# Quantised FFN, first half: groups of four batches in pairs, Gelu over 1,024 columns, row normalisation and quantisation on GpSimd

## The chip, the cores and the metric

The kernel runs on one core of a Trainium2 chip. The metric is the device time of one launch in microseconds; lower is better.

## What is computed

Two layers of a gated cross-attention block over x of 64 x 128 x 128, each an attention and a feed-forward part. The change is in the feed-forward part of the first layer, which works on quantised numbers:

```python
def quantize_a16(x):
    amax = jnp.clip(jnp.max(jnp.abs(x)), 1e-08, None)
    scale = 32767.0 / amax
    x_q = jnp.clip(jnp.round(x * scale), -32768.0, 32767.0) / scale
    return _ste(x, x_q)
W_in_sim = quantize_w8_per(W_in, axis=0)
W_out_sim = quantize_w8_per(W_out, axis=1)
x_sim = quantize_a16(x)
hidden = jax.nn.gelu(x_sim @ W_in_sim + b_in, approximate=False)
hidden_sim = quantize_a16(hidden)
out = hidden_sim @ W_out_sim + b_out
...
x = x + jnp.tanh(g_ffn[0]) * _L0_ffn_ref(_layernorm(x, axis=-1), L0_ffn_W_in, L0_ffn_b_in, L0_ffn_W_out, L0_ffn_b_out)
```

The scale of `hidden` is taken over all of it. So the whole of hidden (512 x 8,192 numbers) must be there before any of it can be quantised, and the part has two halves.

## The kernel before, in words

X, 64 batches of 128 rows by 128 channels, stays in SBUF with rows on the partitions. `quantised_ffn` treats it as 16 groups (`GROUPS`) of four batches (`GROUP`), 512 columns each. There are no loops at run time here: every engine has its own written-out program, and semaphores alone tie them together. Names of the helpers are used below for what they issue.

The **first half** makes HID, `[128, 16, 4, 512]`, the hidden values with their 512 features in four chunks (`FC`) of 128 partitions. For each group g:

- GpSimd, `normalise(g)`: two operations over 512 columns, X minus the row means (`mv`) and times the row's inverse deviation (`rs`), into XN[g % 2] (L1260, L1263). It waits until `quantise(g-2)` has read that buffer.
- VectorE, `quantise(g)`: times the scale `sx`, plus the constant ROUND, which rounds, into XQ[g % 2] (L1386).
- TensorE, `turn(g)`: four transposes into the PSUM bank pX[g % 2] (L1287).
- ScalarE, `high(g)`: a rounded bf16 copy HI of the bank (L1338). VectorE, `low(g)`: the bf16 rest LO (L1392).
- TensorE: for each chunk c two matmuls of 512 columns, W_in by HI and by LO, into the PSUM bank pU[c] (L1304, L1305). One bank per chunk: chunk c of a group waits for the Gelu of the same chunk a group before.
- ScalarE: Gelu with bias and scale from pU[c] into HID (L1351), 512 columns.
- VectorE, `largest(g)`: the largest magnitude of the group's 2,048 columns per partition, into amax (L1397). The last group's is taken chunk by chunk (L1423).

The orders are these. TensorE: turn(g+1), then the four chunks of g. ScalarE: high(g+1), then four Gelus. VectorE: low(g+1), quantise(g+2), largest(g-1). Behind group 1 TensorE also transposes eight blocks of the weights of the second layer's feed-forward part (L1310, L1311). `keep_busy` issues matmuls without use.

After the last group VectorE takes the maximum over amax, TensorE spreads it (`across(1)`) and VectorE makes the scale `sh`. The **second half** quantises HID, multiplies by W_out (L1328) and adds to X. The change leaves it as it is, save that its banks pD now are the two halves of pU[0].

At the start of the stage VectorE finds the largest normalised value from per-row statistics (L1400 to L1404), `across(0)` spreads it and `scale_from(sx)` makes the scale (L1379 to L1381). GpSimd's first `normalise` waits for the third of these steps (`step_`, 3). The five loads of the next attention layer's weights are issued by SyncE at the start.

HALVES is one buffer of 2 x 2,048 columns for XN, XQ, HI, LO and the raw weights; in the second half it holds HQ.

## Time and profile before

| | before |
|---|---|
| median of 3 runs | 1488.27 us (1488.05 to 1488.7) |
| span of the profiled execution | 1487.2 us |
| TensorE busy | 1444.1 us (97%) |
| VectorE busy | 1064.9 us (72%) |
| ScalarE busy | 923.1 us (62%) |
| GpSimd busy | 640.4 us (43%) |

The profiled execution's span runs from its first to its last instruction; the runs' time has about a microsecond around it. The stage of the change stands from 616.2 us to 737.7 us of the span, its first half up to 677.1 us. A row of the timeline gives the start and the length of an instruction, or of several merged ones with their count (x4). Instructions of one engine overlap at their ends, so what one costs in a queue is the distance from its start to the next one's. A bracket tells how long the engine stood idle before it and what released it. PE is TensorE, PEld its weight load, DVE VectorE, ACT ScalarE, POOL GpSimd. The tiles XN, XQ, HI and LO all read HALVES, pX reads u_px and pU reads u_pu.

### The profile page before, as it was taken

What the parts mean: (1) busy time and instruction counts of PE and PEld (TensorE: products, weight loads), DVE (VectorE), ACT (ScalarE), POOL (GpSimd) and SP (SyncE); (2) the same over time, 40 slices, a digit from 0 to 9 for tenths busy, and PEclk for the clock granted to TensorE, in tenths of its full rate; (3) what the DMA queues carried; (4) which work ended last, traced back from release to release, by engine and by line L of the source; (5) the groups of instructions that cost most, each with busy time, mean ns of one, the idle gap of its engine ahead of it and who ended that gap; (6) DMA issues with size and microseconds to landing.
All of it is one profiled execution on the core that took longest, in us unless ns stands there. A gap on an engine that the chain in (4) does not pass through costs nothing. (4 is left out here: it accounts for less than half of the span.)

```text
span 1487.2 us, 27490 instructions
## 1 busy us (share of the span) xinstructions
PE 1444.1 (97%) x9366; PEld 1209.9 (81%) x9384; DVE 1064.9 (72%) x2311; ACT 923.1 (62%) x1924; POOL 640.4 (43%) x755
## 2 busy tenths in 40 slices
PE   9999999999999999879999999999999999999997
PEld 8888888888888887639978888888888888778886
DVE  5677877666767678798566666666767676776887
ACT  4666666666666665496456666666666666556663
POOL 1333344343433334556023434343333333455885
PEclk9999999999999999999999999999999999999999
DMA  7655544444444442300055444444444444320011
GB/s 226 192 178 161 165 132 153 137 145 144 140 146 138 153 130 85 91 1 1 12 183 165 135 157 133 157 129 161 134 159 132 154 129 151 109 79 8 29 35 43
DMA packets 202786, 182.70 MB, mean 123 GB/s; under 512 B 12368, under 2 KB 201808, under 8 KB 202640
## 3 DMA queue, kind: packets, MB, share of 16 engines
q1 hardware_dynamic: 202080, 180.91, 38.7%
q8 instruction: 73, 1.20, 0.3%
q14 instruction: 57, 0.47, 0.1%
q10 hardware_dynamic: 576, 0.13, 0.1%
HBM read 95.74 MB, written 85.25 MB: 122 GB/s over the span
## 5 line engine op out<-in xcount | busy, mean ns | idle before, releaser
L1131 POOL TENSOR_TENSOR PN<-E,RC 128x512 f32<-128x512 f32 x378 | 331.2, 904 | 491.9 <-DVE RC L1089 491.9
L1038 DVE TENSOR_REDUCE MX<-pS 128x6 f32<-128x462 f32 (+1 forms) x384 | 222.6, 580 | 265.4 <-PE pS L657 265.4
L772 ACT ACTIVATE G<-pP 128x308 f32<-128x308 f32 (+1 forms) x488 | 208.9, 428 | 226.8 <-PE pP L525 226.5
L695 PE MATMUL pO<-work,PT 128*128 128x128 f32 (+1 forms) x2560 | 328.3, 276 | 4.1 <-ACT PT L856 4.1
L657 PE MATMUL pS<-G,XT 128*128 128x462 f32 (+1 forms) x768 | 321.0, 507 | 0.0
L695 PEld LDWEIGHTS pO<-work,PT 128*128 128x128 f32 (+1 forms) x2560 | 307.7, 192 | 8.4 <-issue 5.8
L847 ACT ACTIVATE E<-E 128x462 f32<-128x462 f32 (+1 forms) x384 | 209.6, 546 | 136.5 <-DVE E L1048 128.2
L523 PE MATMUL pP<-Chi,Ahi 128*128 128x308 f32 x496 | 235.2, 474 | 1.4 <-ACT G L772 1.2
L1048 DVE TENSOR_TENSOR E<-pS,MX 128x462 f32<-128x462 f32 (+1 forms) x384 | 223.6, 582 | 8.9
L856 ACT ACTIVATE PT<-pT 128x512 f32<-128x512 f32 (+1 forms) x384 | 200.2, 522 | 30.2 <-PE pT L680 28.7
L1086 DVE TENSOR_REDUCE SM<-E 128x16 f32<-128x1232 f32 (+1 forms) x144 | 184.8, 1290 | 44.7 <-ACT E L847 43.6
L680 PE MATMUL pT<-ident,PN 128*128 128x128 f32 (+1 forms) x1280 | 198.7, 273 | 3.7 <-ACT PT L856 3.7
L778 ACT ACTIVATE ST<-pP 128x512 f32<-128x512 f32 x290 | 172.0, 593 | 39.3 <-PE pP L536 36.6
L680 PEld LDWEIGHTS pT<-ident,PN 128*128 128x128 f32 (+1 forms) x1280 | 156.2, 138 | 23.1 <-ACT PT L856 6.0
L657 PEld LDWEIGHTS pS<-G,XT 128*128 128x128 f32 x768 | 137.4, 189 | 32.7 <-issue 15.1
L534 PE MATMUL pP<-Bhi,Vhi 128*128 128x512 f32 x300 | 149.6, 499 | 3.1 <-PEq L160 1.7
L524 PE MATMUL pP<-Chi,Alo 128*128 128x308 f32 x496 | 150.8, 304 | 0.0
L525 PE MATMUL pP<-Clo,Ahi 128*128 128x308 f32 x496 | 150.7, 304 | 0.0
L523 PEld LDWEIGHTS pP<-Chi,Ahi 128*128 128x128 f32 x496 | 94.3, 190 | 30.9 <-issue 21.0
L536 PE MATMUL pP<-Bhi,Vlo 128*128 128x512 f32 x300 | 118.2, 394 | 0.0
L535 PE MATMUL pP<-Blo,Vhi 128*128 128x512 f32 x300 | 118.1, 394 | 0.0
L524 PEld LDWEIGHTS pP<-Chi,Alo 128*128 128x128 f32 x496 | 94.6, 191 | 27.7 <-issue 21.0
(241 smaller groups left out, 2032.7 us busy)
## 6 DMA issues: line engine op xcount, KB each, us to landing
values<-ST SPq DMA_DIRECT2D x256, 256.0 KB
work<-values SPq DMA_DIRECT2D x512, 128.0 KB
values<-ST SPq DMA_DIRECT2D x64, 208.0 KB
work<-values SPq DMA_DIRECT2D x128, 104.0 KB
C<-in_ctx SPq DMA_DIRECT2D x32, 154.0 KB
X<-in_x SPq DMA_DIRECT2D x16, 256.0 KB, 5.0
out<-s_O SPq DMA_DIRECT2D x16, 256.0 KB, 2.3
work<-in_L_xattn_Wq SPq DMA_DIRECT2D x2, 512.0 KB, 5.9
```

The costliest lines, as they stand in the source:

```text
L523: nc.tensor.matmul(out, p["Ahi"][:, head, :], hi, start=True, stop=False)
L524: nc.tensor.matmul(out, p["Alo"][:, head, :], hi, start=False, stop=False)
L657: nc.tensor.matmul(out, XT[:, half, b, :], G[:, half, b, h0:h1, :].rearrange("p h k -> p (h k)"), start=True, stop=True).then_inc(score_re ...
L680: last = nc.tensor.transpose(pT[n % 2][0:rows, c - c0, :], PN[(t - 1) % 2][:, start:start + rows], p["ident"][:, :])
L695: last = nc.tensor.matmul(pO[:, 0:CH], PT[0:rows, c, :], V[(t - 1) % VRING][0:rows, tile, CH * hh:CH * hh + CH], start=c == 0, stop=c == C ...
L772: return nc.scalar.activation(G[0:live, g % 2, :, head, :], bank[0:live, 0:KEYCOLS].rearrange("p (b k) -> p b k", k=KEYS), ACT.Copy)
L847: nc.scalar.activation(e, e, ACT.Exp).then_inc(exp_done, 1)
L856: nc.scalar.activation(PT[0:rows, c0:c1, :], pT[n % 2][0:rows, 0:c1 - c0, :], ACT.Copy).then_inc(p_out, 1)
L1038: nc.vector.tensor_reduce(MX[:, h0:h1], pS[u][:, 0:(h1 - h0) * KEYS].rearrange("p (h k) -> p h k", k=KEYS), X_AXIS, ALU.max).then_inc(max_ ...
L1048: nc.vector.tensor_tensor(E[t % 2][:, h0:h1, :], pS[u][:, 0:(h1 - h0) * KEYS].rearrange("p (h k) -> p h k", k=KEYS), MX[:, h0:h1].unsqueez ...
L1086: last = nc.vector.tensor_reduce(SM[:, h0:h1], E[t % 2][:, h0:h1, :], X_AXIS, ALU.add)
L1131: nc.gpsimd.tensor_tensor(out, e, scale, ALU.mult).then_inc(prob_ready, 1)
```

## The change

The first half goes by pairs of groups, eight of them (`PAIRS`).

- GpSimd's `normalise(g)` is four operations, one per batch, of 128 columns: X plus `minus` (the means, negated once at the start) times `rs`, both read per partition. `quantise(g)` goes to GpSimd too, in place in XQ. Its order: rows of groups 0 and 1, then, after the scale is there, quantise 0 and 1, then rows and quantise of one group after the other. `normalise(g)` waits for turn(g-2).
- TensorE turns groups 0 and 1 first. For each pair a chunk is four matmuls (HI and LO of both groups) into one of two tiles pU[c % 2] of 1,024 columns. A chunk waits for the Gelu two chunks before. Behind chunk 0 stand the turns of the next pair.
- ScalarE's Gelu is over 1,024 columns. Behind the first Gelu of a pair stand both `high` of the next.
- VectorE: both `low` of pair j, then `largest` of both groups of pair j-2. The last pair is reduced chunk by chunk over 1,024 columns.
- HI and LO have four buffers each, XN is gone.

```diff
-        XN = [half_of(0, i, 1).rearrange("p (b d) -> p b d", d=CH) for i in range(2)]
-        XQ = [half_of(0, 2 + i, 1).rearrange("p (b d) -> p b d", d=CH) for i in range(2)]
-        HI = [half_of(1, i, 1).bitcast(BF16)[:, 0:512] for i in range(2)]
+        XQ = [half_of(0, i, 1).rearrange("p (b d) -> p b d", d=CH) for i in range(2)]
+        parts = [half_of(0, 2, 1), half_of(0, 3, 1), half_of(1, 0, 1), half_of(1, 1, 1)]
+        HI = [h.bitcast(BF16)[:, 0:512] for h in parts]
...
-        pU = [s.enter_context(nc.psum_tensor(f"u_pu{i}", [128, 512], F32)) for i in range(FC)]
+        pU = [s.enter_context(nc.psum_tensor(f"u_pu{i}", [128, 2, 512], F32)) for i in range(2)]
...
@@ GpSimd @@
-                if g >= 2:
-                    pool.wait_ge(xq_ready, g - 1)
-                nc.gpsimd.tensor_tensor(XN[half], p["X"][:, rows, :], p["mv"][:, rows, 0:1].to_broadcast([128, GROUP, CH]),
-                                        ALU.subtract).then_inc(centred, 1)
-                pool.wait_ge(centred, g + 1)
-                nc.gpsimd.tensor_tensor(XN[half], XN[half], p["rs"][:, rows].unsqueeze(2).to_broadcast([128, GROUP, CH]),
-                                        ALU.mult).then_inc(xn_ready, 1)
+                if g >= 2:
+                    pool.wait_ge(xq_turned, g - 1)
+                for b in range(GROUP):
+                    t = g * GROUP + b
+                    last = nc.gpsimd.tensor_scalar(XQ[g % 2][:, b, :], p["X"][:, t, :], minus[:, t:t + 1],
+                                                   p["rs"][:, t:t + 1], ALU.add, ALU.mult)
+                last.then_inc(xn_ready, 1)
+
+            def quantise(g):
+                pool.wait_ge(xn_ready, g + 1)
+                nc.gpsimd.tensor_scalar(XQ[g % 2], XQ[g % 2], sx[:, 0:1], ROUND, ALU.mult, ALU.add).then_inc(xq_ready, 1)
 
             nc.gpsimd.sem_clear(range(min(p["spent"]), max(p["spent"]) + 1))
+            nc.gpsimd.tensor_scalar(minus[:, :], p["mv"][:, :, 0], -1.0, 0.0, ALU.mult, ALU.add).then_inc(turned_sign, 1)
             pool.wait_ge(step_, RANGE - 1)
-            for g in range(GROUPS):
+            pool.wait_ge(turned_sign, 1)
+            normalise(0)
+            normalise(1)
+            pool.wait_ge(step_, RANGE + SCALE)
+            quantise(0)
+            quantise(1)
+            for g in range(2, GROUPS):
                 normalise(g)
+                quantise(g)
@@ TensorE @@
             turn(0)
-            for g in range(GROUPS):
-                if g + 1 < GROUPS:
-                    turn(g + 1)
-                pe.wait_ge(hi_out, g + 1)
-                pe.wait_ge(lo_out, g + 1)
+            turn(1)
+            for j in range(PAIRS):
+                for g in (2 * j, 2 * j + 1):
+                    pe.wait_ge(hi_out, g + 1)
+                    pe.wait_ge(lo_out, g + 1)
                 for c in range(FC):
-                    wait(pe, gelu_done, g * FC + c - FC + 1)
+                    wait(pe, gelu_done, j * FC + c - 1)
                     f = slice(128 * c, 128 * c + 128)
-                    nc.tensor.matmul(pU[c][:, :], WIN[:, f], HI[g % 2], start=True, stop=False)
-                    nc.tensor.matmul(pU[c][:, :], WIN[:, f], LO[g % 2], start=False, stop=True).then_inc(up_ready, 1)
-                if g == 1:
+                    for i in range(2):
+                        nc.tensor.matmul(pU[c % 2][:, i, :], WIN[:, f], HI[(2 * j + i) % 4], start=True, stop=False)
+                        last = nc.tensor.matmul(pU[c % 2][:, i, :], WIN[:, f], LO[(2 * j + i) % 4], start=False, stop=True)
+                    last.then_inc(up_ready, 1)
+                    if c == 0 and j + 1 < PAIRS:
+                        turn(2 * j + 2)
+                        turn(2 * j + 3)
+                if j == 0:
@@ ScalarE @@
-            for g in range(GROUPS):
-                if g + 1 < GROUPS:
-                    high(g + 1)
+            for j in range(PAIRS):
                 for c in range(FC):
-                    act.wait_ge(up_ready, g * FC + c + 1)
-                    nc.scalar.activation(HID[:, g, c, :], pU[c][:, :], ACT.Gelu, bias=b_in[:, c:c + 1],
+                    act.wait_ge(up_ready, j * FC + c + 1)
+                    nc.scalar.activation(HID[:, 2 * j:2 * j + 2, c, :], pU[c % 2][:, :, :], ACT.Gelu, bias=b_in[:, c:c + 1],
                                          scale=in_scale[:, c:c + 1]).then_inc(gelu_done, 1)
+                    if c == 0 and j + 1 < PAIRS:
+                        high(2 * j + 2)
+                        high(2 * j + 3)
@@ VectorE @@
-            for g in range(GROUPS):
-                if g + 1 < GROUPS:
-                    low(g + 1)
-                if g + 2 < GROUPS:
-                    quantise(g + 2)
-                if g >= 1:
-                    largest(g - 1)
+            for j in range(1, PAIRS):
+                low(2 * j)
+                low(2 * j + 1)
+                if j >= 2:
+                    largest(2 * j - 4)
+                    largest(2 * j - 3)
+            for g in range(GROUPS - 4, GROUPS - 2):
+                largest(g)
             for c in range(FC):
-                dve.wait_ge(gelu_done, (GROUPS - 1) * FC + c + 1)
-                last = nc.vector.tensor_reduce(amax[:, GROUPS - 1 + c:GROUPS + c], HID[:, GROUPS - 1, c, :],
-                                               X_AXIS, ALU.max, apply_absolute_value=True)
+                dve.wait_ge(gelu_done, (PAIRS - 1) * FC + c + 1)
+                last = nc.vector.tensor_reduce(amax[:, GROUPS - 2 + c:GROUPS - 1 + c], HID[:, GROUPS - 2:GROUPS, c, :],
+                                               mybir.AxisListType.XY, ALU.max, apply_absolute_value=True)
```

The order of the instructions shows it at two places. On VectorE, after the scale is made, there stood before (L1386 `quantise`, L1392 `low`, L1397 `largest`, L1408 and L1413 small operations):

```order
L1386 TENSOR_SCALAR HALVES<-HALVES,sx 128x512
L1408 TENSOR_SCALAR in_scale<-inv,sx 128x4
L1386 TENSOR_SCALAR HALVES<-HALVES,sx 128x512
L1392 SCALAR_TENSOR_TENSOR HALVES<-u_px,HALVES 128x512
L1413 TENSOR_SCALAR gbias_f<-brow_f,gate_f 128x128
L1392 SCALAR_TENSOR_TENSOR HALVES<-u_px,HALVES 128x512
L1386 TENSOR_SCALAR HALVES<-HALVES,sx 128x512
L1392 SCALAR_TENSOR_TENSOR HALVES<-u_px,HALVES 128x512
L1386 TENSOR_SCALAR HALVES<-HALVES,sx 128x512
L1397 TENSOR_REDUCE amax<-HID 128x1
```

and now (L1407 is `low`, L1412 `largest`):

```order
L1422 TENSOR_SCALAR in_scale<-inv,sx 128x4
L1407 SCALAR_TENSOR_TENSOR HALVES<-u_px,HALVES 128x512 x2
L1427 TENSOR_SCALAR gbias_f<-brow_f,gate_f 128x128
L1407 SCALAR_TENSOR_TENSOR HALVES<-u_px,HALVES 128x512 x4
L1412 TENSOR_REDUCE amax<-HID 128x1 x2
L1407 SCALAR_TENSOR_TENSOR HALVES<-u_px,HALVES 128x512 x2
```

The first `largest` stood behind low(0) to low(2), and stands behind low(0) to low(5). On TensorE, from the first turns to chunk 1 of the first pair (L1300 `turn`, L1318 and L1319 the chunks' matmuls, by HI and by LO):

```order
L1300 MATMUL u_px<-ident,HALVES 128x128 x8
L1318 MATMUL u_pu<-HALVES,WIN 128x512
L1319 MATMUL u_pu<-HALVES,WIN 128x512
L1318 MATMUL u_pu<-HALVES,WIN 128x512
L1319 MATMUL u_pu<-HALVES,WIN 128x512
L1300 MATMUL u_px<-ident,HALVES 128x128 x8
L1318 MATMUL u_pu<-HALVES,WIN 128x512
L1319 MATMUL u_pu<-HALVES,WIN 128x512
```

Before, all eight matmuls of group 0 stood ahead of the third turn; now the third and the fourth turn stand ahead of chunk 1.

## Rows read from the trace of the kernel before

**Rows 1.** Windows: start:end, us, busy us of PE, PEld, DVE, ACT, POOL, PEclk, DMA

```profile
620.00:623.50 3.50, 1.28 (x8) 0.83 (x8) 3.49 (x5) 1.05 (x3) 3.34 (x4) 1.00 1.01 304
624.10:627.20 3.10, 3.10 (x11) 1.46 (x10) 1.84 (x2) 2.88 (x5) 2.66 (x3) 0.50 1.20 298
640.00:650.00 10.00, 7.54 (x39) 3.70 (x38) 10.00 (x10) 10.00 (x18) 6.61 (x8) 1.00 0.01 2
```

**Rows 2.** Timeline of one group: start us, us, engine, line, operation

```profile
647.36 0.68 DVE L1392 SCALAR_TENSOR_TENSOR HALVES<-u_px,HALVES 128x512 bf16<-128x512 f32 x1
647.96 0.48 DVE L1386 TENSOR_SCALAR HALVES<-HALVES,sx 128x512 f32<-128x512 f32 x1
648.35 2.28 DVE L1397 TENSOR_REDUCE amax<-HID 128x1 f32<-128x2048 f32 x1
...
649.49 0.83 ACT L1338 ACTIVATE HALVES<-u_px 128x512 bf16<-128x512 f32 x1
...
649.97 3.03 ACT L1351 ACTIVATE HID<-u_pu,b_in,in_scale 128x512 f32<-128x512 f32 x4
...
650.55 0.68 DVE L1392 SCALAR_TENSOR_TENSOR HALVES<-u_px,HALVES 128x512 bf16<-128x512 f32 x1
```

**Rows 3.** Timeline, the end of the first half

```profile
668.80 5.84 ACT L1351 ACTIVATE HID<-u_pu,b_in,in_scale 128x512 f32<-128x512 f32 x8
...
670.26 4.47 DVE L1397 TENSOR_REDUCE amax<-HID 128x1 f32<-128x2048 f32 x2
...
674.65 2.46 DVE L1423 TENSOR_REDUCE amax<-HID 128x1 f32<-128x512 f32 x4
```

**Rows 4.** Waits, 619 to 675: who waited for whom, us in total, times, longest

```profile
POOL HALVES L1260 <- DVE HALVES L1386: 11.7, 12, 1.0
```

**Rows 5.** ScalarE's groups by shape (busy us, mean ns), and the Gelus' ns min/median/max

```profile
L1365 ACT ACTIVATE HALVES<-HID 128x2048 f32<-128x2048 f32 x15 | 28.7, 1914 | 22.5 <-PE u_pu L1328 22.3 <-DVE HID L1437 0.2
...
L1360 ACT ACTIVATE HALVES<-HID 128x512 f32<-128x512 f32 x4 | 2.2, 620 | 3.6 <-DVE HID L1433 3.6
...
L1351 ACT ACTIVATE HID<-u_pu,b_in,in_scale x64: 772/1016/1206, 624.2 to 673.4; 128x512 f32<-128x512 f32 x64
```

**Rows 6.** Timeline, the start of the first half

```profile
617.20 1.04 POOL L1260 TENSOR_TENSOR HALVES<-X,mv 128x512 f32<-128x512 f32 x1 [1.30 <-DVE up L1403]
...
619.53 1.11 DVE L1386 TENSOR_SCALAR HALVES<-HALVES,sx 128x512 f32<-128x512 f32 x1
...
620.70 0.42 PEld L1287 LDWEIGHTS u_px<-ident,HALVES 128*128 128x128 f32 x4 [1.29 <-DVE HALVES L1386]
...
621.39 0.60 ACT L1338 ACTIVATE HALVES<-u_px 128x512 bf16<-128x512 f32 x1 [0.93 <-PE u_px L1287]
...
622.74 0.68 DVE L1392 SCALAR_TENSOR_TENSOR HALVES<-u_px,HALVES 128x512 bf16<-128x512 f32 x1
...
624.20 3.33 ACT L1351 ACTIVATE HID<-u_pu,b_in,in_scale 128x512 f32<-128x512 f32 x4
...
628.24 0.69 DVE L1392 SCALAR_TENSOR_TENSOR HALVES<-u_px,HALVES 128x512 bf16<-128x512 f32 x1 [2.12 <-ACT HALVES L1338]
```

**Rows 7.** Timeline, two matmuls of 512 columns at the full clock

```profile
649.20 0.38 PE L1305 MATMUL u_pu<-HALVES,WIN 128*128 128x512 bf16 x1
...
649.41 0.38 PE L1304 MATMUL u_pu<-HALVES,WIN 128*128 128x512 bf16 x1
```

**Rows 8.** GpSimd: timeline of three casts, and groups by shape (busy us, mean ns)

```profile
35.43 0.40 POOL L140 CAST Vhi<-Chi 128x256 fp32r<-128x256 f32 x1 [8.54 <-DVE Clo L127]
35.78 0.23 POOL L145 CAST Vhi<-Chi 128x52 fp32r<-128x52 f32 x1
35.95 0.41 POOL L140 CAST Vlo<-Clo 128x256 fp32r<-128x256 f32 x1
...
L1263 POOL TENSOR_TENSOR HALVES<-HALVES,rs_after 128x512 f32<-128x512 f32 x16 | 16.8, 1047 | 1.3
...
L1119 POOL TENSOR_TENSOR RS<-VE,half 128x4 f32<-128x4 f32 x32 | 32.3, 1009 | 171.1 <-DVE VE L926 171.1
```

More of the change, by code:

```diff
@@ L1213, in quantised_ffn @@
         brow = sb("brow_f0", [128, CH])
-        amax = sb("amax", [128, GROUPS - 1 + FC])
+        PAIRS = GROUPS // 2
+        amax = sb("amax", [128, 2 * (PAIRS - 1) + FC])
+        minus = sb("minus", [128, BATCH])
         def half_of(i, first, n):
             return HALVES[:, i, 512 * first:512 * (first + n)]
-        XN = [half_of(0, i, 1).rearrange("p (b d) -> p b d", d=CH) for i in range(2)]
-        XQ = [half_of(0, 2 + i, 1).rearrange("p (b d) -> p b d", d=CH) for i in range(2)]
-        HI = [half_of(1, i, 1).bitcast(BF16)[:, 0:512] for i in range(2)]
-        LO = [half_of(1, i, 1).bitcast(BF16)[:, 512:1024] for i in range(2)]
+        XQ = [half_of(0, i, 1).rearrange("p (b d) -> p b d", d=CH) for i in range(2)]
+        parts = [half_of(0, 2, 1), half_of(0, 3, 1), half_of(1, 0, 1), half_of(1, 1, 1)]
+        HI = [h.bitcast(BF16)[:, 0:512] for h in parts]
+        LO = [h.bitcast(BF16)[:, 512:1024] for h in parts]
         raw_fc = half_of(1, 2, 1).rearrange("p (c d) -> p c d", d=CH)
@@ L1227, in quantised_ffn @@
         pX = [s.enter_context(nc.psum_tensor(f"u_px{i}", [128, 512], F32)) for i in range(2)]
-        pU = [s.enter_context(nc.psum_tensor(f"u_pu{i}", [128, 512], F32)) for i in range(FC)]
+        pU = [s.enter_context(nc.psum_tensor(f"u_pu{i}", [128, 2, 512], F32)) for i in range(2)]
         pF = s.enter_context(nc.psum_tensor("pF", [128, 512], F32))
         pP = s.enter_context(nc.psum_tensor("pP", [128, 512], F32))
-        pD = pU[0:2]
+        pD = [pU[0][:, i, :] for i in range(2)]
         gate_in, bias_in, up_bias_in, raw_in, raw_turned, fhi_out = (
             sem(n) for n in ("gate_in", "bias_in", "up_bias_in", "raw_in", "raw_turned", "fhi_out"))
-        centred, xn_ready, xq_ready, xq_turned, hi_out, lo_out, up_ready, gelu_done = (
-            sem(n) for n in ("centred", "xn_ready", "xq_ready", "xq_turned", "hi_out", "lo_out", "up_ready", "gelu_done"))
+        turned_sign, xn_ready, xq_ready, xq_turned, hi_out, lo_out, up_ready, gelu_done = (
+            sem(n) for n in ("turned_sign", "xn_ready", "xq_ready", "xq_turned", "hi_out", "lo_out", "up_ready", "gelu_done"))
         step_, spread, tanh, scaled, gbias_made, biased = (
@@ L1335, in high @@
                 act.wait_ge(xq_turned, g + 1)
-                if g >= 2:
-                    act.wait_ge(up_ready, (g - 1) * FC)
-                nc.scalar.activation(HI[g % 2], pX[g % 2][:, :], ACT.Copy, bias=-ROUND).then_inc(hi_out, 1)
+                if g >= 4:
+                    act.wait_ge(up_ready, (g // 2 - 1) * FC)
+                nc.scalar.activation(HI[g % 4], pX[g % 2][:, :], ACT.Copy, bias=-ROUND).then_inc(hi_out, 1)
             act.wait_ge(gate_in, 16)
@@ L1381, in scale_from @@
                 done(nc.vector.reciprocal(s[:, 0:1], s[:, 1:2]))
-            def quantise(g):
-                dve.wait_ge(xn_ready, g + 1)
-                wait(dve, xq_turned, g - 1)
-                nc.vector.tensor_scalar(XQ[g % 2], XN[g % 2], sx[:, 0:1], ROUND, ALU.mult, ALU.add).then_inc(xq_ready, 1)
             def low(g):
                 dve.wait_ge(hi_out, g + 1)
-                if g >= 2:
-                    dve.wait_ge(up_ready, (g - 1) * FC)
-                nc.vector.scalar_tensor_tensor(out=LO[g % 2], in0=pX[g % 2][:, :], scalar=ROUND, in1=HI[g % 2],
+                if g >= 4:
+                    dve.wait_ge(up_ready, (g // 2 - 1) * FC)
+                nc.vector.scalar_tensor_tensor(out=LO[g % 4], in0=pX[g % 2][:, :], scalar=ROUND, in1=HI[g % 4],
                                                op0=ALU.subtract, op1=ALU.subtract).then_inc(lo_out, 1)
             def largest(g):
-                dve.wait_ge(gelu_done, (g + 1) * FC)
+                dve.wait_ge(gelu_done, (g // 2 + 1) * FC)
                 nc.vector.tensor_reduce(amax[:, g:g + 1], HID[:, g, :, :].rearrange("p c n -> p (c n)"),
@@ L1406, in _ @@
             scale_from(sx)
-            quantise(0)
             nc.vector.tensor_scalar(in_scale[:, :], inv[:, 0, :], sx[:, 1:2], None, ALU.mult).then_inc(scaled, 1)
-            quantise(1)
             low(0)
+            low(1)
             dve.wait_ge(tanh, 1)
```

2 lines of the change are left out of this document (1 added, 1 removed).

## Prediction

> **What bounds the stage now.** The first view is the windows by stretch [rows 1]: from 640 to 650 us VectorE and ScalarE are both busy for all of 10.00 us, TensorE for 7.54 and GpSimd for 6.61. So it has two candidates, and the timeline of one group [rows 2] decides between them. On VectorE one group is `low` (starts 647.36), `quantise` (647.96), `largest` (648.35) and the next `low` (650.55): 0.60 + 0.39 + 2.20 = 3.19 us, without a gap. On ScalarE the next group's `high` starts at 649.49 and its first Gelu at 649.97, so a `high` takes 0.48; Gelus start 0.66 apart where nothing holds them (eight in 5.84 us from 668.80 [rows 3], less 1.21 for the last one's own length, by 7), so a group needs 0.48 + 4 x 0.66 = 3.12. VectorE bounds by 0.07 us, and ScalarE stands right behind it. The waits [rows 4] agree: GpSimd's rows waited 11.7 us for VectorE's `quantise`. The end [rows 3] matters as much: after the last `low` VectorE still has `largest` for groups 13 and 14 (from 670.26) and four quarters of group 15 (from 674.65, 2.46 us together), done at 677.11, and everything behind the stage starts from there. The second half is left alone by the change: it runs out of the same HID, on TensorE, and its transfers were sent long before. A microsecond saved before 677.11 is thus a microsecond of the whole.
>
> **VectorE's work.** Removed: 14 of the 16 `quantise` lie in the loop, at 0.39 each. A pair costs 2 x 0.60 + 2 x 2.20 = 5.60 us, against 6.38. The last pair's four reductions are now over 1,024 columns: 2,048 columns take 2.20 and 512 take 0.60 from start to start, 1.04 ns a column, so 1.13 each. From the start of low(4) on, VectorE has 12 x 0.60 + 14 x 2.20 + 4 x 1.13 + 0.1 for the last one's tail = 42.6 us, and it can't be done before that.
>
> **ScalarE's work.** The copy of 2,048 columns takes 1,914 ns and that of 512 takes 620 [rows 5]: 0.84 ns a column. 512 more columns on a Gelu so add 0.43 to 0.66: 1.09. A pair is 4 x 1.09 + 2 x 0.48 = 5.32, against 6.24.
>
> **TensorE's ring.** Before, a chunk of pU was rewritten four Gelus later; now there are two tiles, so chunk c waits for Gelu c-2. From low's end (622.74 + 0.68) to the first Gelu (624.20) [rows 6] a chunk of two matmuls took 0.78; two more at 0.22 [rows 7] make 1.2, of which about 0.1 is the release. A Gelu of 1,024 lasts 0.77 + 0.43 = 1.20 from start to release (0.77 is the shortest of 512 columns, in the line's rows [rows 5]). Release to release is then (1.20 + 1.1) / 2 = 1.15, not 1.09, where no `high` stands between. With three such steps ScalarE and TensorE need about 5.5 per pair. This still is under VectorE's 5.60.
>
> **GpSimd's work** is the term that the trace doesn't show. Casts of 256 and 52 columns start 0.35 and 0.17 apart [rows 8]: 0.88 ns a column and 0.12 fixed. A 128-column row is at least 0.24, a 512-column `quantise` at least 0.57. The two-input operation took 1.047 for 512 [rows 8]: 1.80 ns a column, so 0.36 and 1.05. I take 0.36 for a row, because it reads two per-partition operands as well, and 0.80 for `quantise`, midway. The far end is the power of four columns, 1.01 [rows 8]: an operation can cost that whatever its width. A pair takes 8 x 0.36 + 2 x 0.80 = 4.5 us (3.1 to 5.0 with the near bounds), hidden under 5.6. Its slack is 1.1; if that goes, `turn` is late and with it everything. The negation of 64 means (about 0.2) stands before the wait on the deviations and is free while they come.
> The Trainium skill (GPSIMD Engine Reference, Performance versus the Vector engine) gives a loop of 1.03 cycles per element up to two operations and about 1.8 beyond, and advises VectorE for elementwise work. By 1.8 cycles a row would be 0.12 + 0.19 = 0.31 and `quantise` 0.89, an estimate from that page; the sum would be the same to 0.2 us.
>
> **The start.** This is where the change pays. All rows of two groups now come before the first `quantise`. GpSimd starts at 617.20 [rows 6]; 8 x 0.36 bring it to 620.1, and the scale has been there since 619.5, when VectorE began its own `quantise`, which ended at 620.64. Two `quantise` end at 620.9 and 621.7. From there turn to `high` 0.69 (620.70, 621.39), `high` 0.60, `low` 0.68, chunk 1.2, handovers 0.1: first Gelu at 624.9, against 624.20: **+0.7**.
> TensorE's order is now chunk 0, then the turns of groups 2 and 3, then chunk 1. GpSimd has them at 621.7 + 2 x (4 x 0.36 + 0.80) + 0.2 for handovers = 626.4. The second turn (0.42) and chunk 1 (1.1) follow: second Gelu at 627.9, 3.0 after the first instead of 2.1. Then Gelus 2 and 3, and the eight transposes of the spiking weights (0.85) stand before pair 1: first Gelu of pair 1 at 632.0. high(4) starts 1.09 later and low(4) 0.65 after that: 633.7. VectorE's first `largest` stands behind low(4) and low(5), though its group is done by 631.6; it has nothing to do from 627 to 633.7. Now it is never idle after 628.24 [rows 6]. End: 633.7 + 42.6 = 676.3, against 677.11: **-0.8 us**.
>
> **The clock.** From 624.1 to 627.2 the granted clock was 0.50, the 1.2 GHz level, after TensorE had been busy for only 1.28 us of the 3.5 from 620 to 623.5 [rows 1], for want of quantised groups. It hardly does more there after the change. If the same stretch is slow again, the first chunk's tail, the turns and chunk 1 take twice as long: four matmuls 0.86 more at either chunk, of which 1.3 us reach low(4). End 677.6, **+0.5 us**. The trace decides for neither, so I put the stage between them: **-0.3 us**. The Trainium skill (TensorE: Matmul & The Clock Gate, What's actually happening) says that activity releases the throttle and lack of it sets it, which speaks for the second value.
>
> The sum is made in the profiled execution, whose span is 1487.2; the median of the runs is 1488.27, 1.1 around it. Forecast: 1488.27 - 0.3 = **1488.0 us**. A measurement of this kernel can tell about 0.2%, 3.0 us, from no change.
>
> **Rivals.**
> - *The saving arrives in full.* VectorE gets low(4) early enough and pays only its work. From 628.24 it then loses 12 x 0.39 = 4.7 us: 1483.6. For it: 11.7 us of waits for `quantise` go [rows 4]. Against it: the order puts the first `largest` behind low(5), and that needs pair 0 finished on ScalarE.
> - *GpSimd becomes the bound.* Place: the rows and `quantise` of a pair, released only by the turns of the pair before. Price: at 0.55 a row, 8 x 0.55 + 2 x 0.80 = 6.0, with two handovers 6.1 per pair. The start slips 3.0 us (8 rows, then 8 more before Gelu 1), and five pairs lose 0.5 each: -0.8 + 3.0 + 2.7 = +4.9, 1493.2. It decides from 0.49 a row on, where 8 rows and two `quantise` fill 5.5. For it: the 1.01 us of four columns; against it: casts are far below. By the Trainium skill's advice on that page this is what moving elementwise work to GpSimd invites; no row here shows it.
> - *The clock stays low through pair 0* because TensorE's work comes in pieces with waits for GpSimd between. Chunks then pass at 1.6 us instead of 1.15 until about 631: 1.1 more on top of the +0.5, 1489.9.
> - *A Gelu of 1,024 saves nothing* (1.32): ScalarE keeps 6.24 per pair and is the bound: +1.9 to +3, about 1490.5. Against it: the fixed part in the copies [rows 5].
>
> **Chances.** Forecast with either clock 0.58 (its own range 1485.6, by 0.24 and 0.57 on GpSimd at full clock, to 1489.0); full saving 0.13; GpSimd bound 0.19; clock low for longer 0.06; Gelu 0.04. The range takes in the forecast's range, part of the full saving and GpSimd up to 0.55 a row: 1484.8 to 1493.5, with 0.1 left out on either side. Faster by over 0.2%: 0.13 and the lower edge of the forecast, 0.16. Slower: 0.19 and half of the last two, 0.24. Within: 0.60.
>
> **What would show it.** Right: `low` and `largest` back to back from low(4) to the end, 5.6 per pair; Gelus 1.1 to 1.2 apart; GpSimd idle about 1 us per pair, a row near 0.36; a VectorE gap of 5 us or more before low(4). Wrong: TensorE waiting for GpSimd's `quantise` in every pair (the second rival), `largest` of group 0 starting before 632 (the first), or a Gelu of 1,024 over 1.2 from start to start.

## The result: 2.0 us slower, where 0.3 us faster was forecast

| | before | changed kernel |
|---|---|---|
| median of 20 runs each, us | 1488.13 (1487.54 to 1489.1) | 1490.13 (1489.22 to 1493.17) |
| ratio, 95% interval | | 1.0015 (1.0009 to 1.0021) |
| profiled execution: time, span, us | 1488.7, 1487.2 | 1493.17, 1491.4 |

The time lies in the forecast's range (1484.8 to 1493.5) and by the median in its band of "within 0.2%", but its sign is wrong: the whole interval of the ratio lies above 1. The profiled execution is the longest of the 20, so its +4.2 us of span shows more than the typical loss; how the two go together is told below.

The page of the changed kernel gives the sums over the span. Neither they nor the chain of what ended last point at the stage:

```profile
PE 1448.6 (97%) x9384; PEld 1212.3 (81%) x9384; DVE 1054.5 (71%) x2294; ACT 917.6 (62%) x1892; POOL 646.0 (43%) x804
```

**The loop is as forecast.** The timeline from 646 us (start, length, engine and line, operation), beside [rows 2]:

```profile
646.47 1.07 ACT L1356 ACTIVATE HALVES<-u_px 128x512 bf16<-128x512 f32 x2
647.10 1.28 DVE L1407 SCALAR_TENSOR_TENSOR HALVES<-u_px,HALVES 128x512 bf16<-128x512 f32 x2
647.42 4.72 ACT L1368 ACTIVATE HID<-u_pu,b_in,in_scale 128x1024 f32<-128x1024 f32 x4
648.30 4.46 DVE L1412 TENSOR_REDUCE amax<-HID 128x1 f32<-128x2048 f32 x2
```

Four Gelus take 4.72, one alone 1.20 or 1.21, so they start 1.17 apart (forecast 1.15 for TensorE's ring). Two `low` and two `largest` fill a pair on VectorE without a gap. The windows, in the columns of [rows 1], show the room on GpSimd, and GpSimd's groups by shape (busy us, mean ns, idle before) show its price, the term that no row of before had:

```profile
640.00:650.00 10.00, 8.16 (x43) 3.88 (x42) 10.00 (x8) 9.93 (x12) 8.90 (x19) 1.00 0.00 0
```

```profile
L1263 POOL TENSOR_SCALAR HALVES<-X,minus,rs_after 128x128 f32<-128x128 f32 x64 | 27.9, 452 | 5.0 <-PE u_px L1300 4.6 <-DVE up L1418 0.3
L1269 POOL TENSOR_SCALAR HALVES<-HALVES,sx 128x512 f32<-128x512 f32 x16 | 11.1, 696 | 1.4
```

A row takes 0.43 from start to start (eight in 3.47 below), a `quantise` 0.68. A pair is 8 x 0.43 + 2 x 0.68 = 4.8 us on GpSimd, under the 5.6 of the others; GpSimd is busy 8.90 us of 10 and never ends a wait in the loop.

**The start** is later than forecast. Timeline from 616 us, against [rows 6]:

```profile
617.16 3.47 POOL L1263 TENSOR_SCALAR HALVES<-X,minus,rs_after 128x128 f32<-128x128 f32 x8 [0.25 <-DVE up L1418]
618.76 0.29 DVE L1399 TENSOR_REDUCE sx<-u_px 128x1 f32<-128x128 f32 x1 [1.45 <-PE u_px L1294]
620.60 1.37 POOL L1269 TENSOR_SCALAR HALVES<-HALVES,sx 128x512 f32<-128x512 f32 x2
626.17 1.21 ACT L1368 ACTIVATE HID<-u_pu,b_in,in_scale 128x1024 f32<-128x1024 f32 x1 [2.86 <-PE u_pu L1319]
627.27 0.71 PEld L1300 LDWEIGHTS u_px<-ident,HALVES 128*128 128x128 f32 x4 [0.77 <-POOL HALVES L1269]
630.14 3.54 ACT L1368 ACTIVATE HID<-u_pu,b_in,in_scale 128x1024 f32<-128x1024 f32 x3 [1.11 <-PE u_pu L1319]
634.21 1.20 ACT L1368 ACTIVATE HID<-u_pu,b_in,in_scale 128x1024 f32<-128x1024 f32 x1 [0.53 <-PE u_pu L1319]
635.93 0.69 DVE L1407 SCALAR_TENSOR_TENSOR HALVES<-u_px,HALVES 128x512 bf16<-128x512 f32 x1 [6.18 <-PE u_pu L1319]
```

The last row is low(4): VectorE stood idle 6.18 us before it, 17.17 us after the scale's first step (618.76). The forecast had 633.7 at full clock. The windows show one reason for the rest: the granted clock was 0.50, the 1.2 GHz level, up to 630. (`e4_start` below, at full clock, prices it at 1.3 us.)

```profile
624.00:626.00 2.00, 1.81 (x5) 0.82 (x6) 0.23 (x2) 0.00 (x0) 2.00 (x5) 0.50 1.18 317
628.00:630.00 2.00, 2.00 (x7) 0.83 (x6) 1.28 (x2) 0.60 (x1) 1.90 (x5) 0.50 0.36 88
```

**The end** holds what the forecast did not look at. Timeline of the changed kernel from 670 us, against [rows 3]:

```profile
670.97 4.40 PE L61 MATMUL u_px<-ident 128*128 128x128 f32 x38
673.82 4.59 DVE L1438 TENSOR_REDUCE amax<-HID 128x1 f32<-128x1024 f32 x4
678.44 0.17 DVE L1442 TENSOR_REDUCE peak<-amax 128x1 f32<-128x18 f32 x1
678.66 0.80 PE L1294 MATMUL u_px<-ident,peak 128*128 128x128 f32 x2 [3.29 <-DVE peak L1442]
679.25 5.33 PE L61 MATMUL u_px<-ident 128*128 128x128 f32 x24
684.37 0.87 PE L1346 MATMUL u_pu<-WOUT,HALVES 128*128 128x128 f32 x5
```

and in the kernel before, up to its first `W_out` matmul (L1328):

```profile
672.46 4.40 PE L61 MATMUL u_px<-ident 128*128 128x128 f32 x38
677.14 0.17 DVE L1427 TENSOR_REDUCE peak<-amax 128x1 f32<-128x19 f32 x1
677.37 0.49 PE L1281 MATMUL u_px<-ident,peak 128*128 128x128 f32 x2 [0.50 <-DVE peak L1427]
677.69 2.84 PE L61 MATMUL u_px<-ident 128*128 128x128 f32 x24
680.37 4.85 PE L1328 MATMUL u_pu<-WOUT,HALVES 128*128 128x128 f32 x42
```

L61 is `keep_busy`: matmuls on an identity, issued to hold the clock, whose result nobody reads. The 38 are the 19 calls that follow the last chunk, the 24 the 12 calls behind the spread. The first set lasts 4.40 us in both kernels, but starts 1.49 us earlier in the changed one, which reaches `peak` 1.30 us later. Then TensorE waits 3.29 us for VectorE's last reductions (0.50 us before the change), and the clock falls: in the changed kernel's windows

```profile
676.00:678.50 2.50, 0.00 (x0) 0.00 (x0) 2.46 (x4) 0.00 (x0) 0.00 (x0) 0.87 0.00 0
678.50:681.00 2.50, 2.34 (x11) 2.34 (x12) 1.44 (x6) 0.20 (x1) 0.00 (x0) 0.50 0.00 0
```

TensorE is idle to 678.66 and at 0.50 from 678.5 on. The same 24 matmuls take 5.33 us instead of 2.84, and the first `W_out` matmul stands behind them.

**The sum of the profiled execution.** From `sx` to `peak`: 678.44 - 618.76 = 59.68, against 677.14 - 618.82 = 58.32 before: +1.36. From `peak` to the next stage's first transpose, 743.11 - 678.44 = 64.67 against 738.97 - 677.14 = 61.83: +2.84. Together +4.2, the difference of the spans.

**How typical it is.** Each run has its mean granted clock over the whole program. Of the 20 runs of the changed kernel five stood at 0.995 or 0.996, at 1491.43 to 1493.17 us; fifteen at 0.997 or 0.998, at 1489.22 to 1490.78. When it was run again (`e11_after`), two of eleven kept 1.000: 1488.94 and 1488.96. The 33 runs of the kernel before beside the first experiments all lie at 0.998 or more, 1487.65 to 1489.39, without such an order. So most of the loss goes with the clock. The two runs at 1.000 are still some 0.6 us above the kernel before (1488.95 against 1488.3); two runs of a rounded mean don't show whether that is there without the clock, and `e5_both` below finds nothing left.

### The profile page after: what moved, and what is told of

Read it like the earlier page. It is cut to its first block and busy times, and to the rows that moved or that the text cites. A ratio compares the mean times of both kernels' runs of the same rounds, so it can differ in the third digit from the quotient of the medians.

```text
span 1491.4 us, 27491 instructions
## 1 busy us (share of the span) xinstructions
PE 1448.6 (97%) x9384; PEld 1212.3 (81%) x9384; DVE 1054.5 (71%) x2294; ACT 917.6 (62%) x1892; POOL 646.0 (43%) x804
```

## The experiments

Two theories at first. **End**: the loss is the clock that falls in TensorE's idle 3.3 us behind the last chunk. **Start**: the loss is the longer way to low(4), through GpSimd's `quantise` and TensorE's low clock. Later a third question: what had the change to give at all. All runs, with the median time of the kernel before on the same chip 1488.42 (`e1` to `e4`), 1488.18 (`e5` to `e8`) and 1488.32 (`e9` to `e12`), and its median span 1486.6, 1486.4 and 1486.5. The last two columns are from the one profiled execution of each, from the scale's first step to `peak` and from `peak` to the next stage's first transpose:

| run | median us | ratio to before (95%) | median span | profile: scale to `peak` | `peak` to next stage |
|---|---|---|---|---|---|
| kernel before | 1488.13 | | | 58.32 | 61.83 |
| changed kernel | 1490.13 | 1.0015 (1.0009, 1.0021) | 1488.3 | 59.68 | 64.67 |
| e11_after | 1490.55 | 1.0016 (1.0007, 1.0025) | 1488.8 | 58.47 | 63.45 |
| e1_busy | 1490.17 | 1.0009 (1.0, 1.0019) | 1487.6 | 59.62 | 61.83 |
| e12_busy | 1490.41 | 1.0008 (0.9999, 1.0017) | 1487.6 | 59.84 | 61.83 |
| e2_early | 1491.66 | 1.002 (1.0011, 1.0029) | 1489.9 | 58.46 | 63.46 |
| e3_vq | 1490.14 | 1.0011 (1.0002, 1.002) | 1488.4 | 57.73 | 61.83 |
| e4_start | 1489.83 | 1.0012 (1.0003, 1.0021) | 1487.7 | 58.38 | 64.54 |
| e5_both | 1488.23 | 1.0003 (0.9994, 1.0012) | 1486.4 | 58.45 | 61.82 |
| e6_stream | 1485.18 | 0.9986 (0.9977, 0.9995) | 1483.0 | 54.66 | 61.84 |
| e7_all | 1483.88 | 0.9971 (0.9961, 0.9981) | 1482.1 | 53.68 | 61.83 |
| e8_pool | 1488.41 | 1.0001 (0.9992, 1.001) | 1486.6 | 57.98 | 61.82 |
| e9_groups | 1486.25 | 0.9986 (0.9977, 0.9995) | 1484.5 | 55.82 | 61.87 |
| e10_bfill | 1488.48 | 1.0001 (0.9992, 1.001) | 1486.4 | 57.65 | 61.82 |

The time around the span was 1.8 us in most runs, but 2.1 to 2.5 in the median of `e1`, `e4`, `e6`, `e10` and `e12`. (The "about a microsecond" ahead of the prediction, and the prediction's 1.1, compare the span of one execution, whose time was 1488.7, with the median of others.) Where less than 1 us matters the median span is therefore read beside the time. The span has a scatter of its own too: what lies outside the two stretches of the last columns adds up to 1366.0 to 1367.1 us in the fourteen profiles, whatever the kernel. So the spans of single profiles can't settle 1 us; the two columns leave this scatter out.

### e1_busy and e12_busy: fill the hole at the end

```diff
-            keep_busy(nc, p, spare, 19)
+            keep_busy(nc, p, spare, 32)
```

> The changed kernel with 32 instead of 19 matmuls without use behind the last chunk, nothing else. Theory: VectorE still ends the first half at 678.4 us, so amax is not earlier, but TensorE now works until it is needed. The granted clock stays at the full level from 678.5 to 684 us (0.50 there in the changed kernel), the 12 matmuls behind the spread take 2.8 us and not 5.3, and the first matmul by W_out starts 2.5 to 2.8 us sooner. Median 1488.3 to 1488.8 us, and the runs lie closer together than the changed kernel's 1489.2 to 1493.2. Rival (the loss lies in the loop, where GpSimd or the ring of two PSUM tiles sets the pace): 1490.1, no change.

> The first run once more (32 matmuls without use at the end, nothing else), since its profile showed the clock full and its median did not move. Theory: the median lies 1 to 2 us below that of the changed kernel run beside it. Rival (the filling at the end helps only when the start is filled as well): equal within 0.5 us, as in the first set.

In the windows of `e1_busy` the clock at the end is full, and the timeline has the 24 matmuls back at their old length:

```profile
678.00:680.00 2.00, 1.59 (x15) 1.59 (x15) 1.21 (x6) 0.00 (x0) 0.00 (x0) 1.00 0.00 0
```

```profile
678.73 2.84 PE L61 MATMUL u_px<-ident 128*128 128x128 f32 x24
```

In this profile the fill does what it was meant for: TensorE is kept busy and the clock stays. From `peak` to the next stage it is 61.83 us again, as before the change. The table says the same of all the kernels: 61.8 to 61.9 us in the ten profiles that kept full clock behind `peak`, 63.4 to 64.7 in the four that lost it. The size in the time is less plain. The median hardly moved (1490.17 and 1490.41, where 1488.3 to 1488.8 was expected, and for the second 1 to 2 us below the changed kernel), the ratio fell by 0.0006 to 0.0008, and the median span by 0.7 and 1.2 us; no run was left at a clock of 0.996 or less. Two runs of the same edit gave the same median span, 1487.6, and I take about 1 us for it. By the time alone the rival, equal within 0.5 us, holds; the difference between the two is the time around the span, whose growth I can't explain.

### e4_start: fill the waits at the start

```diff
-            keep_busy(nc, p, spare, 4)
+            keep_busy(nc, p, spare, 12)
             turn(0)
             turn(1)
+            keep_busy(nc, p, spare, 5)
```

> The changed kernel with 8 more matmuls without use behind the first spread and 5 behind the second turn, so that TensorE does not stand idle before the first pair. Theory of the clock at the start: the granted clock stays full from 624 to 630 us (0.50 in the changed kernel), chunk 0 takes 1.2 and not 2.0 us, chunk 1 likewise, low(4) comes 1.3 us sooner and the end too: median 1488.6 to 1489.0. Rival (GpSimd's quantise of group 3 sets the start whatever the clock): the second Gelu moves by under 0.5 us.

```profile
624.00:626.00 2.00, 1.40 (x11) 1.02 (x11) 1.12 (x3) 0.20 (x1) 1.90 (x4) 1.00 1.13 330
628.00:630.00 2.00, 1.83 (x11) 1.12 (x12) 1.14 (x2) 0.87 (x2) 1.90 (x6) 1.00 0.78 188
678.00:680.00 2.00, 1.75 (x8) 1.75 (x9) 0.91 (x5) 0.00 (x0) 0.00 (x0) 0.50 0.00 0
```

These are its windows: full clock at the start, 0.50 still at the end. The timeline has low(4) 15.88 us after the scale instead of 17.17:

```profile
635.52 1.29 DVE L1408 SCALAR_TENSOR_TENSOR HALVES<-u_px,HALVES 128x512 bf16<-128x512 f32 x2 [5.34 <-PE u_pu L1320]
```

VectorE's work behind low(4) is the same 42.5 us (635.52 to 678.02; in the changed kernel 635.93 to 678.44), so all of the 1.3 us reaches `peak`: 58.38 us after the scale. The median span falls by 0.6 us. Again the profile shows the mechanism, and by the median spans it is worth 0.6 to 1.1 us alone, about half of the loss. The median time, 1489.83, missed the expected 1488.6 to 1489.0.

### e5_both: both holes

The two diffs above in one kernel.

> The changed kernel with both fillings of TensorE's idle stretches at once (8 and 5 matmuls without use at the start, 32 instead of 19 at the end). Theory: with the clock full throughout, the first half ends as long after the scale's first step as in the kernel before (58.3 to 58.4 us), and the second half starts undisturbed: median 1488.2 to 1488.8 us, runs within 1 us of each other. Rival (the scatter from 1489.2 to 1493.2 comes from something other than the clock at these two places, such as GpSimd's pace): the median stays at 1489.8 or above and the runs stay 2 us or more apart.

1488.23 beside 1488.18: nothing is left of the loss in the median. The median spans are equal, 1486.4. The windows of the stage show 1.00 everywhere. Since the interval of this ratio (up to 1.0012) overlaps those of the changed kernel (from 1.0009, and from 1.0007 in `e11_after`), the spans decide here: 1488.3 to 1488.8 without the fill, 1487.6 and 1487.7 with one, 1486.4 with both. The loss against the kernel before is the clock, at both ends of the stage, in about equal parts. One part of the expectation failed: the runs were to lie within 1 us of each other and are 2.7 us apart (1487.46 to 1490.17), two of them at a clock of 1.000 with 1489.2 and 1489.69. The kernel before scatters by 1.8 us beside them. So the scatter of single runs is in part something other than this clock; what, is open.

### e3_vq: the first two `quantise` back on VectorE

```diff
-            pool.wait_ge(step_, RANGE + SCALE)
-            quantise(0)
-            quantise(1)
...
+                if g == 2:
+                    pool.wait_ge(xq_ready, 2)
...
+            quantise(0)
             nc.vector.tensor_scalar(in_scale[:, :], inv[:, 0, :], sx[:, 1:2], None, ALU.mult).then_inc(scaled, 1)
+            quantise(1)
```

> The changed kernel with quantise of groups 0 and 1 given back to VectorE, which waits there. Theory (the start on GpSimd costs: 3.5 us of rows, 1.4 us of quantise): the first Gelu comes 0.5 to 1 us sooner than 626.2, the second 1 to 1.5 us sooner than 630.1, since GpSimd is at the rows of group 2 1.4 us earlier; low(4) at 634.6 to 635.2 and the end of the first half as much earlier. Median 1489.0 to 1489.6. Rival (the clock alone sets the start): under 0.3 us.

In its timeline low(4) comes 15.23 us after the scale (618.44), though the clock was at 0.50 from 624 to 626:

```profile
625.03 1.20 ACT L1367 ACTIVATE HID<-u_pu,b_in,in_scale 128x1024 f32<-128x1024 f32 x1 [2.71 <-PE u_pu L1318]
633.67 1.29 DVE L1410 SCALAR_TENSOR_TENSOR HALVES<-u_px,HALVES 128x512 bf16<-128x512 f32 x2 [5.34 <-PE u_pu L1318]
...
676.40 0.49 PE L1293 MATMUL u_px<-ident,peak 128*128 128x128 f32 x2 [3.31 <-DVE peak L1447]
676.72 2.84 PE L61 MATMUL u_px<-ident 128*128 128x128 f32 x24
```

Its first Gelu starts 6.59 us after the scale, that of the changed kernel 7.41. Its profiled execution, at 1487.79, happened to keep the full clock at the end; its runs spread from 1487.79 to 1491.73, with two at a clock of 0.996. The median, 1490.14, was expected at 1489.0 to 1489.6 and doesn't show the shorter start. The end's hole is still there to take it back, and the two runs at 0.996 are the slowest; but two runs at 0.999 took 1490.65 and 1490.93, so the clock doesn't order these runs, and why the median stands where it does is not shown. TensorE was idle for 3.31 us ahead of the second spread in this profile too, and the clock stayed at 1.00 behind it: such a stretch does not bring the clock down every time.

### e2_early: less work in VectorE's tail, a miss

The first pair was reduced by chunks ahead of low(4), so that every later `largest` would stand a pair nearer to its Gelus.

```diff
             for j in range(1, PAIRS):
+                if j == 2:
+                    for c in range(FC):
+                        dve.wait_ge(gelu_done, c + 1)
+                        nc.vector.tensor_reduce(amax[:, c:c + 1], HID[:, 0:2, c, :], mybir.AxisListType.XY, ALU.max,
+                                                apply_absolute_value=True)
                 low(2 * j)
                 low(2 * j + 1)
-                if j >= 2:
+                if j >= 3:
```

> The changed kernel with the two reductions of the first pair taken chunk by chunk ahead of low(4), where VectorE waited 6.2 us. Theory (VectorE's work behind low(4), 42.5 us, sets the end): low(4) stays at 635.9, the end of the first half comes 4.4 us sooner, at 674.0, TensorE's matmuls without use cover the gap again, the clock stays full: median about 1485.3 us, 0.2% faster than the kernel before. Rival (GpSimd or the ring sets the pace): the last Gelu already ends at 672.3, so up to 4 us could come from the order alone only if VectorE was the bound; if the pace is set elsewhere the end moves by under 1 us and the median stays at 1489 to 1490.

```profile
634.91 1.29 DVE L1407 SCALAR_TENSOR_TENSOR HALVES<-u_px,HALVES 128x512 bf16<-128x512 f32 x2 [0.83 <-ACT HALVES L1356]
640.49 1.29 DVE L1407 SCALAR_TENSOR_TENSOR HALVES<-u_px,HALVES 128x512 bf16<-128x512 f32 x2 [4.29 <-PE u_pu L1319]
646.08 1.28 DVE L1407 SCALAR_TENSOR_TENSOR HALVES<-u_px,HALVES 128x512 bf16<-128x512 f32 x2
```

The wait only moved: 4.29 us of idle VectorE came ahead of low(6), because nothing was put behind low(5) in the place of what was drawn forward. The lag of a pair at the end was unchanged, TensorE was idle for 3.3 us there as before, and the median is the worst of all. (Why it is above the changed kernel's is not shown; six of its eleven runs stood at 0.995 or 0.996.) One thing is learned: low(6) comes 5.58 us after low(4) although VectorE stood idle for 4.29 us between them, so the ring of ScalarE and TensorE sets 5.58 by itself. This is one interval; from 640.49 on VectorE is busy throughout. VectorE's own work in a pair is the same 5.58: the two are level, and VectorE can never make up in the loop what it is late by at the start.

### e6_stream and e7_all: VectorE takes each chunk when it is there

```diff
-                low(2 * j)
-                low(2 * j + 1)
-                if j >= 2:
-                    largest(2 * j - 4)
-                    largest(2 * j - 3)
...
+            for j in range(PAIRS):
+                if j + 1 < PAIRS:
+                    low(2 * j + 2)
+                    low(2 * j + 3)
+                for c in range(FC):
+                    n = j * FC + c
+                    dve.wait_ge(gelu_done, n + 1)
+                    last = nc.vector.tensor_reduce(amax[:, n:n + 1], HID[:, 2 * j:2 * j + 2, c, :],
+                                                   mybir.AxisListType.XY, ALU.max, apply_absolute_value=True)
```

`e6_stream` has this with the start of `e4_start` and 17 calls of `keep_busy` at the end; `e7_all` adds the edit of `e3_vq` and keeps 4 calls ahead of the first turn.

> As the run before, but VectorE reduces each pair chunk by chunk (1,024 columns) right behind the low of the next pair, so it never lags a pair behind; 17 matmuls at the end since the wait there is shorter. Theory (the end is set by VectorE's lag of four reductions of 2,048 columns, 8.8 us behind the last low): the last reduction now ends 1.3 to 2.5 us after the last Gelu, near 673.5, 3.5 us sooner than e5's: median 1484.7 to 1485.5. Rival (the ring of two tiles and ScalarE set the end): VectorE's last reduction would end no sooner, since the last Gelu ends at 672.3 in the changed kernel; then under 1 us.

> e6 with quantise of groups 0 and 1 on VectorE (and only 4 matmuls ahead of the first turn, 5 behind the second). Theory: the start is 1.3 to 1.9 us shorter, as the third run of the first set showed, and this adds to e6: median 1483.2 to 1484.2. Rival (the clock and the start are the same microsecond counted twice): no better than e6 by more than 0.5 us.

Timeline of `e6_stream`:

```profile
628.82 4.59 DVE L1431 TENSOR_REDUCE amax<-HID 128x1 f32<-128x1024 f32 x4
634.24 1.29 DVE L1408 SCALAR_TENSOR_TENSOR HALVES<-u_px,HALVES 128x512 bf16<-128x512 f32 x2 [0.84 <-ACT HALVES L1357]
635.45 4.59 DVE L1431 TENSOR_REDUCE amax<-HID 128x1 f32<-128x1024 f32 x4
...
663.95 9.09 DVE L1431 TENSOR_REDUCE amax<-HID 128x1 f32<-128x1024 f32 x8
673.08 0.19 DVE L1435 TENSOR_REDUCE peak<-amax 128x1 f32<-128x32 f32 x1
```

VectorE's idle 6 us ahead of low(4) now holds the first pair's four reductions, and behind the last `low` stand eight of 1.13 us instead of 8.8 + 4.6 us. A pair costs 5.70 us (639.95 and 645.65 are the next two `low`), 0.12 more than in the changed kernel, and still `peak` comes 54.66 us after the scale instead of 58.45 (`e5_both`). Its median is 1485.18 us, but three of its eleven runs took 1487.74 to 1489.21 at a clock of 0.999, which is not explained. With `quantise` on VectorE for the first two groups it is 53.68, and `e7_all` is at 1483.88 us (nine runs, 1482.92 to 1485.38), ratio 0.9971 (0.9961 to 0.9981), ahead of both kernels. So a time like the one that the forecast gave a chance of 0.13 (1483.6) can be reached, with three things that the change did not have: the streamed order (3.4 us of median span, `e5_both` to `e6_stream`), the first two `quantise` on VectorE (a further 0.9), and the fill of TensorE's holes.

### e8_pool and e9_groups: which part of the change gives it

`e8_pool` is the kernel before with the rows and `quantise` on GpSimd and nothing else; groups stay single, a Gelu has 512 columns.

```diff
-                if g + 2 < GROUPS:
-                    quantise(g + 2)
```

`e9_groups` adds the streamed reduction over 512 columns and 12 calls of `keep_busy` at the end.

> One part of the change alone, in the kernel before: rows by 128-column operations and quantise on GpSimd, with Gelu over 512 columns, four PSUM banks, orders of TensorE and ScalarE as before. Theory (what cost time is the pairing: two groups' rows, turns and lows ahead of the first Gelu, and VectorE's lag at the end): the first Gelu stays at 624.2, ScalarE is the bound at 3.12 per group, VectorE has 2.80, so it keeps up and the first half ends about 0.7 us after the last Gelu, at 674.0: median 1485.0 to 1485.8. Rival (GpSimd's share is what costs): slower than the kernel before by 1 us or more.

> No pairs at all: the kernel of the GpSimd part alone, with VectorE reducing each chunk of 512 columns of a group right behind the low of the next, and 12 instead of 19 matmuls without use at the end. It tells what the pairs are worth once the order of VectorE is the good one. Theory (ScalarE's 3.16 us per group is then all that is left; its last Gelu ends near 674.3): the first half ends about 675.0, 1.9 us sooner than without the new order: median 1486.2 to 1486.8, 1 to 1.5 us behind the paired kernel in that order (1485.2). Rival (the gain of that kernel is VectorE's order alone and the pairs give nothing): 1485.2 or less.

`e8_pool` was a miss: no change at all (1488.41). Its timeline:

```profile
646.78 3.01 ACT L1362 ACTIVATE HID<-u_pu,b_in,in_scale 128x512 f32<-128x512 f32 x4
647.14 0.69 DVE L1398 SCALAR_TENSOR_TENSOR HALVES<-u_px,HALVES 128x512 bf16<-128x512 f32 x1 [0.28 <-ACT HALVES L1349]
647.75 2.27 DVE L1403 TENSOR_REDUCE amax<-HID 128x1 f32<-128x2048 f32 x1
...
669.87 4.47 DVE L1403 TENSOR_REDUCE amax<-HID 128x1 f32<-128x2048 f32 x2
```

VectorE now waits 0.28 us per group for ScalarE, and a group takes 3.16 (650.31 less 647.14 for the next `low`) against 3.19 [rows 2]. Taking `quantise` from VectorE gives almost nothing while ScalarE stands right behind, and GpSimd's share costs nothing either. The two `largest` at the end stand there as in [rows 3]. `e9_groups` takes away that lag as well and gets 1486.25, as expected; its profile also had full clock at the start, where that of `e8_pool` had 0.50 from 624 to 626, so not all of the 2.2 us between their 57.98 and 55.82 need be the order's. So by median spans against the kernel before: GpSimd's share alone +0.2 (`e8_pool`), with streamed reductions -2.0 (`e9_groups`), and with pairs and Gelus of 1,024 columns -3.4 (`e6_stream`). The last step of 1.4 is not the pairs' alone, since `e6_stream` also has the filled start and `e9_groups` does not.

### e10_bfill: did the kernel before lose time at its start too?

```diff
-            keep_busy(nc, p, spare, 4)
+            keep_busy(nc, p, spare, 8)
             turn(0)
+            keep_busy(nc, p, spare, 6)
```

> Control for the filling of the start: the kernel before with 4 more matmuls without use ahead of its first turn and 6 behind it. Theory (the low clock at the start delays turn 2, and with it low(2), after which VectorE is never idle): low(2) comes about 1 us sooner than 628.2, the median is 1487.0 to 1487.4. Rival (only the paired order is sensitive to that clock, since VectorE bounds the kernel before): 1488.2, no change.

From the scale to `peak` it took 57.65 instead of 58.32, so full clock is worth 0.7 us there in the profile; but the median did not move (1488.48 against 1488.32, where 1487.0 to 1487.4 was expected), and the median span only by 0.1. In its profile the scale itself came 0.6 us later (619.43 against 618.82). The added matmuls are not the cause, for they stand behind the spread that it waits for, and `e6_stream`, with as many ahead of its first turn as `e4_start`, has 618.42; this point lies between 618.4 and 619.7 in all the profiles. At equal, full clock the changed kernel's first half thus takes 58.45 - 57.65 = 0.8 us more than that of the kernel before, in the profiled executions; the median spans, 1486.4 for both, don't show it.

### e11_after: the changed kernel once more

> The changed kernel once more, beside the others on this chip. Theory: the first half ends 59.6 to 59.7 us after the scale's first step (58.3 in the kernel before), TensorE stands idle for 3 us ahead of the second spread, and the granted clock is 0.50 behind it; median 1490.1. Rival (the clock there falls only in some executions): the profile shows full clock behind the spread and a span of about 1488.5.

1490.55, the ratio 1.0016 again. Its profiled execution took 58.47 us from the scale to `peak`, where 59.6 to 59.7 was expected, because it had another clock: low(4) 15.97 us after the scale and 0.50 only for part of the time at the start (0.73 from 626 to 628), and at the end

```profile
677.75 4.47 PE L61 MATMUL u_px<-ident 128*128 128x128 f32 x24
```

4.47 us where the first profile had 5.33 and the kernel before 2.84. How long the low clock lasts differs from execution to execution, at both places. The Trainium skill (TensorE: Matmul & The Clock Gate, What's actually happening) says that throttled is the default, that activity releases it, and that the same kernel shows different numbers of slow matmuls in different runs; the changed kernel's two profiles agree, with the same 24 matmuls in 5.33 and 4.47 us.

## Why the prediction failed, step by step

- **VectorE's work.** Right: 42.6 us forecast behind low(4), 42.5 measured in every run with this order; a pair 5.60, measured 5.58.
- **ScalarE and TensorE's ring.** Right in kind, a little small: 1.15 forecast, 1.17 measured; "about 5.5 per pair" is 5.58. The forecast's "This still is under VectorE's 5.60" is not so: they are level, which changed nothing here.
- **GpSimd.** A row 0.43 for 0.36, `quantise` 0.68 for 0.80; a pair 4.8 for 4.5. "It decides from 0.49 a row on" was not reached. The slack of 1.1 was 0.6 to 0.8, and the second rival fell. (Its price counted 2.7 for five pairs at 0.5, which is 2.5. The prediction's estimate by 1.8 cycles took the rate that it gives itself for more than two operations; a row and a `quantise` have two each.)
- **The start.** The forecast had the scale at 619.5 and q(1) at 621.7; two `quantise` from 620.60, 1.37 long, end at 621.97. First Gelu 624.9 or, with the low clock's 0.86, 625.8, measured 626.17. GpSimd's 626.4 for the turn of group 3 was 627.27. Low(4) 633.7 or 635.0, measured 635.93. With full clock (`e4_start`, the scale 0.88 later) it is 635.52, 634.6 if moved to the changed kernel's scale: 0.9 above the forecast's 633.7. Sixteen rows at 0.43 for 0.36, less four `quantise` at 0.68 for 0.80, make 0.6 of it; the rest I put down to the handovers.
- **The clock at the start.** "The trace decides for neither, so I put the stage between them." The price of 1.3 was right: 17.17 against 15.88. It applied to the profiled execution in full and in `e11_after` in small part (15.97). The forecast of -0.3, between -0.8 and +0.5, took in only 0.5 of the 1.3, so it is up to 0.8 us too low here.
- **The step that failed, a term put at nothing: "done at 677.11, and everything behind the stage starts from there ... The second half is left alone by the change."** The forecast followed VectorE to its end and did not ask what TensorE does meanwhile. TensorE and ScalarE finish sooner than before, VectorE does not, and its tail behind the last `low` grew: so TensorE, with 19 calls of filler, stands idle for 3.3 us. Behind it lies work at half the clock, filler first, that the first `W_out` matmul must wait for. The term was put at nothing and measured 2.84 us in the profiled execution, 1.62 in `e11_after`, and about 1 us in the median span (`e1_busy`, `e12_busy`). From the order of the code and the rows of before this could have been worked out: a tail of 8.8 + 4.6 us behind the last pair's `low`, four chunks of 1.15 and 4.4 us of filler against it. The sign does not hang on this step alone: the start, with 0.9 us of work and 1.3 of clock, had already made the 0.8 us forecast faster at `peak` into 1.36 slower.
- **The chances.** "Within 0.2%" had 0.60 and holds (+0.15% by the ratio, 0.09 to 0.21). The sign within it was open, and I had let the saving (0.8 us at full clock) lead. With the two clock terms as measured the steps give -0.8 + 0.9 (start) + 1.3 (clock at the start) + 2.8 (clock at the end) = +4.2, the profiled execution's own.

That the time lies in the range is therefore no merit of the mechanism; the range was made wide for GpSimd, which did not become the bound.

Still open: why the time around the span is up to 0.7 us longer in the median of five of the kernels, why single runs scatter by 2 us and more even at full clock, and why at a start like this the clock recovers at 627 in one execution and at 630 in another.

## What to carry to other kernels

When a change shortens the work of TensorE but not that of the engine which ends the stage, look for the idle hole that opens between them: price the work behind it at half clock, filler included, and size the filler again. Before taking work from a bounding engine, look at what it still has to do behind the last input: here the order of VectorE's reductions was worth 2 to 3.5 us, and taking `quantise` away without it nothing.

## What the hardware showed that I had not expected

- GpSimd's `tensor_scalar` takes 0.43 us for 128 columns (two per-partition operands) and 0.68 for 512 (one, and a constant). If the operands make no difference, which no run isolates, that is 0.65 ns a column and 0.35 fixed. Casts had shown 0.88 and 0.12 [rows 8]; with narrow rows it would be the fixed part that counts.
- Filler is not free where it stands ahead of real work: at 1.2 GHz the 24 matmuls behind `peak` cost 2.5 us more on the path to `W_out` than at 2.4 GHz.
- VectorE's `in_scale` of four columns took 1.00 us in the kernel before and in `e10_bfill`, where GpSimd ran its two-input operations, and 0.22 to 0.43 in the changed kernel and all its variants, `e8_pool` and `e9_groups` too, where it ran one-input ones. No run changes that alone, so the cause is not shown.
